# Macaron block (routed experts, Mamba mixer, routed experts): order of tile copies and second expert matrices on VectorE at the start of each expert loop

## What is computed

```python
x = x + 0.5 * moe(layernorm(x))
x = x + mamba_block(layernorm(x))
x = x + 0.5 * moe(layernorm(x))
```

```python
logits = xt @ Wr + br
top_vals, top_idx = jax.lax.top_k(logits, 2)
gate = softmax over the two chosen logits, zero elsewhere
h = relu(einsum('td,edh->teh', xt, W1) + b1)
y = einsum('teh,ehd->ted', h, W2) + b2
out = einsum('ted,te->td', y, gate)
```

## Time and profile before

| what | us |
| --- | --- |
| runs of the kernel (3) | 416.44, 417.07, 419.63 |
| median of the runs | 417.07 |
| the profiled execution | 421.09 |
| its span | 419.3 |
| mean granted TensorE clock in it | 0.901 |

### The profile page before, as it was taken

The page is one execution under the profiler, slowest core; times in us unless marked ns, Lnnn a source line. Parts: engine busy times, 40 slices in busy tenths (PEclk is TensorE's granted clock), DMA queues, the critical chain, the costliest instruction groups (busy, mean ns, idle before and its releaser), DMA issues.

```text
span 419.3 us, 8909 instructions
## 1 busy us (share of the span) xinstructions
PE 330.8 (79%) x2366; PEld 294.6 (70%) x2366; DVE 269.0 (64%) x920; ACT 209.8 (50%) x501; POOL 220.7 (53%) x263
## 2 busy tenths in 40 slices
PE   8784799986698198799999999749469998778800
PEld 7684799976697185567777779739459998767700
DVE  4883477753465178768788986899447775345416
ACT  3832456644464065736657573453245665455402
POOL 4026355566545177274656879651644556654512
PEclk9578899999899598899999999877899999899965
DMA  6791111111111410000000000010111111111154
GB/s 161 239 283 45 27 39 42 40 44 44 41 33 33 172 48 2 1 0 2 1 2 3 0 0 2 2 74 28 52 31 39 38 41 45 41 40 38 33 172 147
DMA packets 18674, 22.23 MB, mean 53 GB/s; under 512 B 4114, under 2 KB 13508, under 8 KB 18628
## 3 DMA queue, kind: packets, MB, share of 16 engines
q1 hardware_dynamic: 13092, 11.18, 8.9%
q0 software_dynamic: 4096, 8.40, 6.7%
q10 hardware_dynamic: 1440, 2.11, 1.4%
HBM read 14.33 MB, written 7.34 MB: 52 GB/s over the span
## 4 chain that ended last, share of the span: by engine, by line
PE 51%; DVE 11%; issue 9%; DMA 6%; SPq 6%; ACT 5%; POOL 4%; another core or an unknown queue 3%; DVEq 3%; ACTq 0%; POOLq 0%
PE PS L793 16%; PE PS L805 16%; SPq L401 3%; PE PS L842 3%; PE PS L849 3%; PE PS L896 2%; PE PS L814 2%; PE PS L778 2%; DMA YT_all<-y_rows 2%; SPq L395 2%; DMA y_rows<-YS,rows_out 2%; DVE X L1507 2%; POOL rs L501 2%; DVE YT_all L1475 1%
## 5 line engine op out<-in xcount | busy, mean ns | idle before, releaser
L479 POOL DMA_INDIRECT XG<-xn_rows,rows_in x64 | 62.1, 970 | 83.8 <-issue 35.7
L793 PE MATMUL PS<-XT_all,W1B 128*128 x624 | 90.1, 290 | 15.8 <-DVE XT_all L1454 8.0
L793 PEld LDWEIGHTS PS<-XT_all,W1B 128*128 128x128 f32 x624 | 80.3, 201 | 18.9 <-issue 18.2
L1121 ACT ACTIVATE H<-PS,W1B 128x128 f32<-128x128 f32 x156 | 48.7, 363 | 88.9 <-PE PS L793 60.7
L489 POOL DMA_INDIRECT y_rows<-YS,rows_out x64 | 62.3, 974 | 48.3 <-issue 18.9
L805 PE MATMUL PS<-H,W2B 128*128 128x128 f32 x624 | 85.3, 281 | 0.5 <-issue 0.5
L805 PEld LDWEIGHTS PS<-H,W2B 128*128 128x128 f32 x624 | 78.4, 197 | 0.9 <-issue 0.6
L1484 DVE COPY W2B<-W2S 128x513 f32 x78 | 35.5, 455 | 39.1 <-DVE YT_all L1475 26.6
L1111 ACT ACTIVATE W1B<-W1S 128x516 f32 x78 | 49.4, 633 | 21.7 <-issue 9.0
L1475 DVE TENSOR_SCALAR YT_all<-PS,W2B 128x128 f32 x78 | 27.2, 349 | 43.3 <-PE PS L805 25.8
L1465 DVE TENSOR_SCALAR H<-PS,W1B 128x128 f32<-128x128 f32 x156 | 46.9, 342 | 6.4 <-PE PS L793 3.8
(11 more groups left out here) (204 smaller groups left out, 556.0 us busy)
## 6 DMA issues: line engine op xcount, KB each, us to landing
YT_all<-y_rows SPq DMA_DIRECT2D x8, 512.0 KB, 5.1
W1S<-in_L_ffn_W SPq DMA_DIRECT2D x1, 2048.0 KB
W2S<-in_L_ffn_W SPq DMA_DIRECT2D x8, 256.0 KB
xn_rows<-XN ACTq DMA_DIRECT2D x8, 256.0 KB, 4.4
X<-in_L_attn_x SPq DMA_DIRECT2D x4, 256.0 KB, 4.7
XG<-xn_rows,rows_in POOLq DMA_INDIRECT x64
y_rows<-YS,rows_out POOLq DMA_INDIRECT x64
out_x<-X SPq DMA_DIRECT2D x4, 256.0 KB, 2.3
```

Of the source, the lines that this page charges most:

```text
L479: g.indirect_dma_start(out=XG[:, u, :], out_offset=None, in_=xn_dram, in_offset=bass.IndirectOffsetOnAxis(ap=rows_in[:, i:i + 1], axis=0), ...
L793: last = mm(PS[2 + 2 * half + j % 2][:, c * P:(c + 1) * P], W1B[w][:, h * P:(h + 1) * P], XT_all[:, ds(start, P)], start=True, stop=True)
L1121: last = A(H[w][:, 2 + c, :], PS[4 + j % 2][:, c * P:(c + 1) * P], ACT.Relu, bias=W1B[w][:, HID + 2 + c:HID + 3 + c])
```

## The change

DVE no longer makes the three W2B copies ahead of its loop. In the loop, steps -2, -1 and 0 now make the copies for steps 0, 1 and 2, each at the step's end: behind the copy of the transposed tile, and in step 0 also behind `add_bias(0)`. The copy for step 3 stays in step 0, directly behind it. The other engines' programs, all waits and all buffers are as before.

```diff
-                for j in range(TRIO):
-                    second_weights_of(j)
                 for step in range(-2, SLOT_TILES):
                     if 0 <= step + 1 < SLOT_TILES:
                         relu(step + 1)
...
                         copy_xt(g)
                     if step >= 0:
                         add_bias(step)
-                        if step + TRIO < SLOT_TILES:
-                            second_weights_of(step + TRIO)
+                    if step < 1:
+                        second_weights_of(step + 2)
+                    if 0 <= step and step + TRIO < SLOT_TILES:
+                        second_weights_of(step + TRIO)
```

## The result

| comparison | changed kernel, us | kernel before, us | ratio, 95% interval |
| --- | --- | --- | --- |
| first (22 runs each) | 420.44 | 417.75 | 1.0072 [1.0046, 1.0097] |
| e13 (12 and 20 runs) | 426.81 | 424.23 | 1.0075 [1.0042, 1.0108] |
| e6 (12 and 19 runs) | 402.85 | 403.85 | 0.9982 [0.9964, 0.9999] |
| e11 (12 and 23 runs) | 401.83 | 403.26 | 0.9965 [0.9942, 0.9988] |

The times are medians of all executions; the ratio and its interval leave out the executions more than 1.5% above the fastest of the same kernel.

A forecast was written before the change was run, and what follows sets the result against it. The prediction took PE (TensorE) as the bound, with DVE's order setting its early waits. Gains 1.7 + 3.0 + 1.4 - 1.5 + 0.4 = 5.0 us, off the 417.07 median, gave 412.0 us; range 406.5 to 418.0.

The forecast's parts named there:

- What bounds the kernel now: Whole kernel: PE bounds, busy 330.8 of 419.3 us with 51% of the last chain; DVE's order sets PE's early waits.
- rival D: Expert loops: early gain given back before the layer ends, through gathers not landed or the scatter queue; 416.5 us, chance 0.17.
- Each later step follows PE ... so I carry it to the end whole: Steps after the first ones: they follow PE, so the whole 5.0 us gain lasts to the end.
- What is open: late results of PE: down(0) to add_bias(0): result 3.5 and 3.9 us late in layers 0 and 1; 0.2 us per layer taken as gain.
- Rival C: add_bias(0) stays at 43.85 and 307.64, early start lost, W2B(2) costs 0.77 per layer; 418.6 to 420.4 us, chance 0.13.
- What is removed: the wait of the first up: First up matmul of each layer: tile copied before W2B, so up(0) starts 1.7 and 3.0 us earlier.
- What goes with it: the clock: up(1) in both layers: less PE idleness keeps the full clock, gaining 0.9 + 0.5 = 1.4 us.
- What is added where PE waits: Ahead of up(3): W2B(2) behind add_bias(0) delays the tile copy 0.77 us per layer, 1.5 us back.
- the extra stretch of 0.2 per layer: Moved W2B copies: beside GpSimd instructions they would stretch by 0.2 us each, making the gain 4.6 rather than 5.0.

The follow-up runs named there:

- e13: The changed kernel once more, nothing else altered, against the kernel before: 426.81 us beside 424.23, ratio 1.0075.
- e6: The changed kernel, unaltered, run for its trace against the kernel before: 402.85 us beside 403.85, ratio 0.9982.
- e11: The changed kernel once more, unaltered, against the kernel before: 401.83 us beside 403.26, ratio 0.9965.
- quick setting: Not one run: the four of six sets of runs in which the kernel before took 403 to 404 us.
- late setting: Not one run: the two of six sets of runs in which the kernel before took 418 to 424 us.
- e14: The changed kernel with each gather from the fourth tile on waiting for the transpose four tiles before, against the kernel before: 427.59 us, ratio 1.0089.
- e18: The changed kernel with W2B(2) ahead of add_bias(0) instead of behind it, against the kernel before: ratio 0.9973.
- e7: The changed kernel with W2B(2) ahead of add_bias(0) instead of behind it, against the kernel before: 401.93 us, ratio 0.9949.
- e17: The kernel before with gathers left out, SyncE loading plain rows instead, against the kernel before: 388.44 us, ratio 0.9657.

## Why the prediction was wrong

**What bounds the kernel now** named PE alone, by busy time and chain. In the quick setting it is POOL's row of transfers that sets the length of both expert loops. Rows 7 had the sign of it: gathers at 1.69 us with 0.75 between them. I read them for rival D and gave it 0.17.

**"Each later step follows PE ... so I carry it to the end whole"** is the step that failed in the quick setting. The gain at up(3) was 0.5 us in layer 0 and 4.1 in layer 1 of e6 and came to 0.6 and 1.2 at the last scatter; in e11 it was 3.8 and 4.2 and came to 1.4 and 0.9. Rival D (the gain taken back by gathers not landed and by the scatter queue) is what the traces show, with 1.0 to 1.4 us left of the 5.

**What is open: late results of PE** is the step that failed in the late setting, the one forecast for. I took 0.2 us per layer, on the ground that both layers show the lateness "at the same step". It goes with POOL's stretch of gathers, not with the step: with PE ahead it fell on tile 1 and relu(1), in layer 1 on tile 2, and add_bias(0) stayed near its time, at 15.1 and 15.9 us behind the first gather, until pacing moved it to 10.7 and 9.7 (e14). So the early start of 1.9 and 2.8 us bought nothing, where the sum had carried all of it and added 0.4. I had also read add_bias(0) of the kernel before as free and waiting since down(0); it stood behind the copy of tile 2, which was late itself.

Rival C had the start lost in this way, with 43.60 inside its condition (43.5 or later) and prices of 418.6 to 420.4. That its price meets the 420.44 is luck as far as these traces show: it put the loss on W2B(2), and behind add_bias(0) that cost 0.5 and 0.6 us, while at up(4) the changed kernel is 0.5 us ahead in layer 0 and 0.6 behind in layer 1. PE did run at half clock in up(2) of layer 1 after 5.36 us of idleness. But the profiled executions sum to the same, and where the median's 3 us arise stays open. Executions vary by 7 to 11 us in this setting; that the changed kernel meets more late results fits (51.0 us of such waits on DVE and ACT against 35.0, one trace of each) and is not proved.

**What is removed: the wait of the first up** held: behind the first gather up(0) is 1.9 and 2.8 us earlier in the first comparison, 1.5 and 2.7 in the quick setting, for 1.7 and 3.0. In layer 1 up(0) began 0.31 us behind the end of the tile copy (293.48), inside the 0.14 + 0.2 of the sum. The profile names ACT's W1B there, but the first of its three copies began at 291.68 and took 0.63, so what filled the 0.31 us is not shown.

**What goes with it: the clock** held in layer 1 (up(1) 1.15 instead of 1.66; 0.5 as taken, 0.9 in the quick setting). In layer 0 of the first comparison it did not. The windows:

```profile
35.00:36.00 1.00, 0.02 (x1) 0.00 (x0) 0.12 (x1) 0.00 (x0) 0.92 (x1) 1.00 0.23 74
38.00:39.00 1.00, 0.79 (x3) 0.79 (x4) 0.51 (x2) 0.00 (x0) 0.42 (x1) 0.50 0.13 41
```

The granted clock was 1.00 early in the idle stretch ahead of up(1) and 0.50 behind it, the level of the earlier trace rows, so the late result took the clock along with the time. In the quick setting it differs from trace to trace: with 1.18 us of idleness ahead of up(0) in layer 0 each time, up(0) and up(1) took 2.07 us in e6 and e18 and 1.15 in e11 and e7. So the 0.9 us taken there came in some executions and not in others, and the short idleness does not decide it.

**What is added where PE waits** was a little too large. The two copies start 0.83 and 0.82 us apart for 0.77. But from the start of add_bias(0) to the tile copy behind relu(2) DVE took 1.91 us before in both layers and 2.45 and 2.53 after, 0.5 and 0.6 more, since the one copy before had been stretched to 0.64 and 0.65. In the quick setting the whole 0.77 is there (the wait of 1.19 against 0.43).

The Trainium skill's "SBUF: two separate sides" (SBUF — State Buffer) lets such a copy and a GpSimd instruction exclude each other. The trace agrees in part: of three W2B copies of the changed kernel that began while a gather instruction ran (33.76, 294.03, 306.46), two took 0.43 us and one 0.64, so the extra stretch of 0.2 per layer that I had allowed for did not come on top.

## What to carry to other kernels

An engine that issues indirect transfers back to back can bound a loop at 55% busy: add the gap ahead of each issue to its duration, multiply by the count, and compare the product with the length of the loop, before a gain on another engine is carried to the end. A wait whose releaser the trace cannot name, on a result whose row has long ended, may belong to the stretch of time and not to the step; it should be priced both ways until an experiment has moved it. And a change worth under 1% should be timed in several sets of runs before its sign is believed: here it turned between two settings of the same program.

## What the runs showed of the hardware

- The same kernel before took 403.1, 403.9, 403.3 and 403.6 us in four sets of runs and 417.8 and 424.2 in two. The traces of the late setting show PE's results noticed late, with waits of up to 6.4 us, most of them while POOL issues transfers in a row; none of the eleven traces of the quick setting with gathers shows one. The last two sets were recorded under the same chip number, with 424.2 us in one and 403.6 in the next, so it may come and go on one chip. What it is remains open.
- A gather of 128 rows costs POOL 1.25 us where no wait on PE stands ahead of it in the program and 1.69 where one does (0.94 and a gap of 0.30 or 0.75), also where the wait has long been met. Pacing moved the change from gather 8 to gather 4 (e14: 1.69 us from 32.47 to 34.16). The scatters of layer 1 of e6 average 1.57, those of the late setting 1.72 to 1.84.
- TensorE's granted clock after a stretch of idleness differs between executions of one kernel: up(0) behind 1.18 us of idleness took 2.07 us in e6 and 1.15 in e11, and in layer 1 of e17 it took 1.15 behind 2.87 us of idleness.
